# Value and output weights of a cross attention multiplied in split form

## The chip, the cores and the metric

The kernel runs on one core of a Trainium2 chip. The metric is the device time of one execution in microseconds (us); lower is better.

## The reference, cut to what matters

The program is one layer: a gated cross attention (stage "a" of the kernel), a causal self attention (stage "b") and a mixture of experts (stage "m"). The change lies in stage a, which computes this:

```python
q = rmsnorm((layernorm(x) @ Wq) per head, gq)      # 16 heads of 128, 1024 tokens
k = rmsnorm((ctx @ Wk) per head, gk)
v = (ctx @ Wv) per head
attn = softmax(q k^T / sqrt(128))                  # 16 sequences of 64 tokens
out = concat(attn @ v) @ Wo
x = x + tanh(g_xattn) * out
```

Since attn @ (ctx @ Wv) @ Wo equals (attn @ ctx) @ (Wv @ Wo), the kernel multiplies Wv of a head by Wo of that head (128x128 by 128x256) once, and applies the product, called vo, to attn @ ctx.

## The kernel before

The 1024 tokens are done in two halves of 512. A stage runs over eight pairs of heads for each half: first stage a for half 0 and half 1, then stage b twice, then stage m twice. Each engine has its own program (`cross_pair(u)` for a pair u of stage a), and semaphores tie them together. The programs are pipelined: in the body of pair u, TensorE makes the scores of u, the attention output of the pair before (`prev`) and the queries and keys of the next one (`nxt`), and VectorE and GpSimd already split the weights of the one after (`after`).

**Split form.** Most matmuls take their operands as two float32r tiles, `hi` (the value rounded by a copy) and `lo` (the rest, raw minus hi). A product is then three matmuls: hi by hi, hi by lo and lo by hi. On GpSimd the helper `rest` (L1470) makes every `lo`. The product of value and output weights is not made so: `value_out` (L629 to L636) multiplies the loaded float32 tiles as they are, one matmul for each head, into `bank_k`. It is made only in the bodies of half 0 (`u.weighs_values`), so eight times; ScalarE (`take_value_out`) and VectorE (`split_value_out`) then turn it into `vo_hi` and `vo_lo`, which stay for half 1.

**The order in a body of stage a.** TensorE: norm_q, scores(u), context_values(prev), keys of nxt, queries of nxt (head 0), keys (head 1), output(prev, head 0), queries (head 1), output(prev, head 1), value_out(u), norm_k(nxt), turn_attn(u). output waits for `pv_lo`. ScalarE: root_k, log_q, root_q, take_context_values(prev), take_k, exponentials(u), squares of the keys and queries, take_value_out, log_k, take_rows. VectorE: scale_scores(u) (L1230, L1233, L1239), subtract_max (L1244), `pv_lo` of prev (L1215), normalise(u) (L1250 to L1254), then queries and casts of weights, split_value_out. GpSimd: rest of the key squares of nxt (`sq_k_lo`), then rests of the query and key weights of `after`.

**Loads.** SyncE issues all the weight loads of stage a. `raw_a2` of a head holds Wv and Wo of that head (192 KB), and is loaded for the next pair once `value_out` has read it; behind it in the queue stands `reload_a1`, the load of the query and key weights two pairs on.

Of the kernel before, what the change touches and what calls it, by code (L numbers as in the profile page):

```python
# [29 lines left out]
ACT = mybir.ActivationFunctionType  # L30
AX = mybir.AxisListType.X

P = 128
# [160 lines left out]
def flamingo_layer(nc, x, ctx_t, ctx, head_a, head_b, pair_v, chunk_m, small, out, shared_units):  # L194
    TOK, D = x.shape
# [35 lines left out]
    with ExitStack() as stack:  # L231
# [94 lines left out]
        def stage_sems(tag, names):  # L326

            return {n: sem(f"{tag}_{n}") for n in names.split()}

        A = stage_sems("a", "wq_hi wq_lo wk_hi wk_lo q_done k_done sq_q sq_k sq_k_hi sq_k_lo qt kt scores raw scaled max "  # L330
                       "sub exp sum inv norm t_done attn_t vo_done vo_hi vo_lo ssk_done ssq_done ln_q "
                       "ln_k r_k r_q pv_done pv_hi pv_lo wo_done")

# [70 lines left out]
        def _(sp):  # L404
# [59 lines left out]
                load_m2(Unit(plan, "m", 0, h))  # L464
            for n in range(1, HALVES * PAIRS):
                if n < PAIRS:
                    sp.wait_ge(A["vo_done"], n)
                    for h in range(2):
                        load_a2(numbered("a", n), h)
                if n + 2 < HALVES * PAIRS:  # L470
                    reload_a1(n + 2)
# [42 lines left out]
        def _(pe):  # L514
# [114 lines left out]
            def value_out(u):  # L629

                pe.wait_ge(A["kt"], u.of(1) + 2)
                for h in range(2):
                    pe.wait_ge(ld_a2[h], 16 * u.n)
                    last = nc.tensor.matmul(bank_k[:, h * D:(h + 1) * D], raw_a2[h][:, AV:AV + C], raw_a2[h][:, AO:AO + D],
                                            start=True, stop=True)
                last.then_inc(A["vo_done"], 1)  # L636

            def norm_q(u):
# [204 lines left out]
        def _(act_e):  # L843
# [124 lines left out]
            def take_head_values(u, h):  # L968
                act_e.wait_ge(B["pv_done"], u.of(h))
                nc.scalar.activation(pv_hi[:, h], value_bank(h)[:], ACT.Copy).then_inc(B["pv_hi"], 1)  # L970

            def take_value_out(u):
                act_e.wait_ge(A["vo_done"], u.n)
                nc.scalar.activation(vo_hi[:, 2 * u.i:2 * u.i + 2, :], bank_k[:].rearrange("p (h n) -> p h n", h=2),
                                     ACT.Copy).then_inc(A["vo_hi"], 1)
# [16 lines left out]
            def cross_pair(u):  # L992

                prev, nxt = u.prev(), u.next()
                root_k(u)
                log_q(u)
                root_q(u)
                if prev:
                    take_context_values(prev)
                take_k(nxt, 0)  # L1000
                exponentials(u)
                if nxt.kind == "a":
                    square_k(nxt, 0, sq_k, A["sq_k"])
                    square_k(nxt, 0, sq_k_hi, A["sq_k_hi"])
                    take_k(nxt, 1)
                    square_k(nxt, 1, sq_k, A["sq_k"])
                    square_k(nxt, 1, sq_k_hi, A["sq_k_hi"])
                    square_q(nxt, 0)
                prepare(u)
                if nxt.kind == "a":  # L1010
                    square_q(nxt, 1)
                    if u.weighs_values:
                        take_value_out(u)
                    if u.very_first:
                        split_context(1)
                    prepare(u, 1)
                    log_k(nxt)
                take_rows(u)
                if nxt.kind != "a":
                    take_v(nxt, False)  # L1020
                    take_context_values(u)
                    take_k(nxt, 1)
# [443 lines left out]
        @block.gpsimd  # L1466
        def _(pool):
            def rest(lo, raw, hi, signal):

                nc.gpsimd.tensor_tensor(lo, raw, hi, ALU.subtract).then_inc(signal, 1)  # L1470

            def split_queries(u, h):
                if u.kind == "a":
                    pool.wait_ge(A["wq_hi"], u.of(h))
                    rest(wq_lo[h][:], raw_a1[h][:, AQ:AQ + D], wq_hi[h][:], A["wq_lo"])
                else:
                    pool.wait_ge(B["wq_hi"], u.of(h))
                    rest(wq_lo[h][:], raw_b1[h][:, 0:D], wq_hi[h][:], B["wq_lo"])

            def split_keys(u, h):  # L1480
                if u.kind == "a":
                    pool.wait_ge(A["wk_hi"], u.of(h))
                    rest(wk_lo[h][:, 0:P], raw_a1[h][:, AK:AK + P], wk_hi[h][:, 0:P], A["wk_lo"])
                else:
                    pool.wait_ge(B["wk_hi"], u.of(h))
                    rest(wk_lo[h][:], raw_b1[h][:, D:2 * D], wk_hi[h][:], B["wk_lo"])

            def split_gate_and_up(u):
                pool.wait_ge(M["wg_hi"], u.done())
                rest(wq_lo[u.parity][:], raw_m1[u.parity][:, MG:MG + D], wq_hi[u.parity][:], M["wg_lo"])  # L1490
                pool.wait_ge(M["wu_hi"], u.done())
                rest(wk_lo[u.parity][:], raw_m1[u.parity][:, MU:MU + D], wk_hi[u.parity][:], M["wu_lo"])

            def split_down(u):
                pool.wait_ge(M["wd_hi"], u.done())
                rest(wo_lo[u.parity][:], raw_m2[u.parity][:], wo_hi[u.parity][:], M["wd_lo"])

            def split_head(after, h):

                if after.kind == "m":  # L1500
                    split_gate_and_up(after.next() if h else after)
                else:
                    split_queries(after, h)
                    split_keys(after, h)

            def split_values(u):
                pool.wait_ge(B["wv_hi"], u.n)
                rest(wv_lo[:], raw_v[:], wv_hi[:], B["wv_lo"])

            def split_out(u, h):  # L1510
                pool.wait_ge(B["wo_hi"], u.of(h))
                rest(wo_lo[h][:], raw_b2[h][:], wo_hi[h][:], B["wo_lo"])

            def split_squares(u, h):
                pool.wait_ge(A["sq_k"], u.of(h))
                pool.wait_ge(A["sq_k_hi"], u.of(h))
                rest(sq_k_lo[:, h], sq_k[:, h], sq_k_hi[:, h], A["sq_k_lo"])

            def cross_pair(u):
                nxt = u.next()  # L1520
                after = nxt.next()
                if nxt.kind == "b":
                    split_values(nxt)
                if nxt.kind == "a":
                    for h in range(2):
                        split_squares(nxt, h)
                for h in range(2):
                    split_head(after, h)
                if u.very_first:
                    pool.wait_ge(ctxt_hi_ready, HALVES)  # L1530
                    rest(ctxt_lo[:, HT:TOK], ctxt[:, HT:TOK], ctxt_hi[:, HT:TOK], ctxt_lo_ready)

            def self_pair(u):
                nxt = u.next()
                after = nxt.next()
                if nxt.kind == "b":
                    split_values(nxt)
                    split_head(after, 0)
                for h in range(2):
                    split_out(u, h)  # L1540
                if nxt.kind == "b":
                    split_head(after, 1)

            def chunk(u):
                nxt = u.next()
                after = nxt.next() if nxt else None
                if u.very_first:
                    split_down(u)
                if after:
                    split_gate_and_up(after)  # L1550
                if nxt:
                    split_down(nxt)

            nc.gpsimd.memset(zeros[:].bitcast(F32), 0.0).then_inc(setup_pool, 1)
            nc.gpsimd.memset(ones[:], 1.0).then_inc(setup_pool, 1)
            nc.gpsimd.memset(attn_t[:], 0.0).then_inc(setup_pool, 1)
            nc.gpsimd.memset(eps5[:], 1e-5).then_inc(setup_pool, 1)
            nc.gpsimd.memset(eps6[:], 1e-6).then_inc(setup_pool, 1)
            nc.gpsimd.memset(ones_of[:].bitcast(F32), 0.0).then_inc(setup_pool, 1)
            pool.wait_ge(setup_pool, SETUP - SPB)  # L1560
            for s in range(SPB):
                nc.gpsimd.memset(ones_of[:, s, s * SEQ:(s + 1) * SEQ].bitcast(F32), 1.0).then_inc(setup_pool, 1)
            start = plan.first_of(0)
            for h in range(2):
                split_head(start, h)
            for h in range(2):
                split_squares(start, h)
            for h in range(2):
                split_head(start.next(), h)
            bodies = {"a": cross_pair, "b": self_pair, "m": chunk}  # L1570
            for kind, half in STAGES:
                run_units(pool, kind, half, bodies[kind])
# [70 lines left out]
```

## Time and profile before

| | us |
|---|---|
| median of 3 runs | 691.06 |
| lowest and highest | 689.58, 694.18 |
| profiled execution, whole time | 690.55 |
| its span, first to last instruction | 688.8 |
| TensorE busy in the span | 668.5 |
| VectorE busy | 470.1 |
| ScalarE busy | 340.9 |
| GpSimd busy | 297.5 |

The profile is of one execution; outside its span lie 1.75 us. Its mean granted TensorE clock is 0.998 of full speed. Times of a row are counted from the begin of the span. Stage a of half 0 runs from some 20 to 125 us, with a body each 13.07 us where nothing else is put beside it. Two bodies are longer, 13.79 us from 70.84 and 13.93 us from 84.63, as VectorE prepares the tokens of the second half in them; the first one is 11.60 us. A body is counted here from the start of its first VectorE instruction (`sc_sub` L1230).

### The profile page before, as it was taken

How to read it: one execution, taken by the hardware profiler on the slowest of the kernel's cores; microseconds unless marked ns; L12 is line 12 of the kernel's file. 1: busy time of each engine (PE TensorE's matmuls, PEld its weight loads, DVE VectorE, ACT ScalarE, POOL GpSimd, SP SyncE). 2: the span in 40 equal slices, each digit the busy share in tenths (PEclk: the TensorE clock that was granted, in tenths of full speed). 3: DMA queues.
4: the chain of work that ended last, by engine and by line, in shares of the span. 5: the costliest groups of instructions: out<-in, count | busy, mean ns of one | idle time of the engine just before them, and what ended most of it. 6: DMA issues, size and time to landing. Idle time of an engine off the chain costs nothing.

```text
span 688.8 us, 14632 instructions
## 1 busy us (share of the span) xinstructions
PE 668.5 (97%) x5415; PEld 585.9 (85%) x5415; DVE 470.1 (68%) x885; ACT 340.9 (49%) x689; POOL 297.5 (43%) x371
## 2 busy tenths in 40 slices
PE   7899999999999999999999999999998999999997
PEld 5688878887888899888989989888887988888886
DVE  5677877678786658676566668846556787655555
ACT  5676666676673333433353433354447444444443
POOL 4434224334334243434333335434553666655553
PEclk9999999999999999999999999999999999999999
DMA  6511311100102122222222212012332223332332
GB/s 205 178 47 52 88 47 48 48 25 24 43 6 57 44 86 63 78 62 62 78 87 68 77 47 77 31 32 70 91 93 87 74 83 92 102 92 91 91 91 92
DMA packets 35866, 50.08 MB, mean 73 GB/s; under 512 B 4064, under 2 KB 22880, under 8 KB 35808
## 3 DMA queue, kind: packets, MB, share of 16 engines
q1 hardware_dynamic: 35376, 48.89, 23.9%
q8 instruction: 39, 0.64, 0.4%
q10 hardware_dynamic: 432, 0.39, 0.2%
q14 instruction: 19, 0.16, 0.1%
HBM read 48.22 MB, written 1.05 MB: 72 GB/s over the span
## 4 chain that ended last, share of the span: by engine, by line
PE 75%; DVE 15%; ACT 5%; issue 2%; DMA 1%; POOL 1%; SPq 0%; DVEq 0%; ACTq 0%; POOLq 0%
PE acc L548 21%; PE bank_q L521 11%; PE bank_k L521 10%; PE bank_v L624 7%; PE bank_v L521 6%; PE bank_s L670 5%; PE bank_s L521 4%; PE bank_p L701 2%; PE bank_t L701 2%; PE bank_q L645 2%; DVE pv_lo L1215 2%; PE bank_p L656 2%; PE bank_t L678 2%; DVE sc L1233 2%; DVE sc_max L1239 2%
## 5 line engine op out<-in xcount | busy, mean ns | idle before, releaser
L548 PE MATMUL acc<-wo_hi,pv_hi 128*128 128x256 f32 x328 | 95.0, 290 | 2.6 <-DVE pv_lo L1335 2.1
L548 PE MATMUL acc<-wo_lo,pv_hi 128*128 128x256 f32 x328 | 93.1, 284 | 0.0
L548 PE MATMUL acc<-wo_hi,pv_lo 128*128 128x256 f32 x328 | 92.8, 283 | 0.0
L1470 POOL TENSOR_TENSOR sq_k_lo<-sq_k,sq_k_hi 128x512 fp32r<-128x512 f32 x32 | 42.2, 1320 | 105.3 <-ACT sq_k_hi L915 105.3
L1470 POOL TENSOR_TENSOR wq_lo<-raw_m,wq_hi 128x256 fp32r<-128x256 f32 x50 | 44.1, 882 | 65.4 <-DVE wq_hi L1291 61.2
L548 PEld LDWEIGHTS acc<-wo_hi,pv_hi 128*128 128x128 f32 x328 | 62.1, 189 | 6.8 <-issue 2.9
L548 PEld LDWEIGHTS acc<-wo_lo,pv_hi 128*128 128x128 f32 x328 | 62.4, 190 | 1.8
L1335 DVE TENSOR_TENSOR pv_lo<-rows_t,pv_hi 128x512 fp32r<-128x512 f32 (+1 forms) x51 | 36.8, 723 | 39.1 <-ACT pv_hi L990 39.1
L990 ACT ACTIVATE pv_hi<-rows_t 128x512 fp32r<-128x512 f32 (+1 forms) x51 | 31.7, 623 | 63.6 <-DVE rows_t L1330 62.0
L548 PEld LDWEIGHTS acc<-wo_hi,pv_lo 128*128 128x128 f32 x328 | 62.5, 191 | 0.0
L911 ACT ACTIVATE kt<-bank_k 128x512 f32<-128x512 f32 x64 | 38.0, 594 | 44.9 <-PE bank_k L521 44.9
L1470 POOL TENSOR_TENSOR wq_lo<-raw_b,wq_hi 128x256 fp32r<-128x256 f32 x32 | 24.5, 764 | 82.2 <-DVE wq_hi L1275 82.2
L521 PE MATMUL bank_q<-xt_hi,wq_hi 128*128 128x512 f32 x146 | 59.7, 409 | 0.1
L1322 DVE TENSOR_TENSOR r_k<-ln_k,unit_w 128x512 f32<-128x512 f32 x44 | 32.7, 743 | 37.7 <-ACT ln_k L981 37.5
L521 PE MATMUL bank_q<-xt_hi,wq_lo 128*128 128x512 f32 x146 | 57.5, 394 | 0.0
L521 PE MATMUL bank_q<-xt_lo,wq_hi 128*128 128x512 f32 x146 | 57.4, 393 | 0.0
L1470 POOL TENSOR_TENSOR wk_lo<-raw_m,wk_hi 128x256 fp32r<-128x256 f32 x50 | 41.3, 827 | 32.2 <-ACT wk_hi L1059 32.2
L521 PE MATMUL bank_k<-xt_hi,wk_hi 128*128 128x512 f32 x114 | 46.4, 407 | 0.0
L947 ACT ACTIVATE ex<-sc_sub 128x512 f32<-128x512 f32 x32 | 20.2, 632 | 52.1 <-DVE sc_sub L1244 52.1
L521 PE MATMUL bank_k<-xt_lo,wk_hi 128*128 128x512 f32 x114 | 44.9, 394 | 0.0
L521 PE MATMUL bank_k<-xt_hi,wk_lo 128*128 128x512 f32 x114 | 44.8, 393 | 0.0
L548 PE MATMUL acc<-vo_hi,pv_hi 128*128 128x256 f32 x128 | 37.7, 294 | 5.8 <-DVE pv_lo L1215 5.8
(203 smaller groups left out, 1985.2 us busy)
## 6 DMA issues: line engine op xcount, KB each, us to landing
raw_m<-in_chunk_m SPq DMA_DIRECT2D x50, 256.0 KB, 2.7
raw_a<-in_head_a SPq DMA_DIRECT2D x48, 192.0 KB, 2.6
raw_b<-in_head_b SPq DMA_DIRECT2D x32, 256.0 KB, 3.0
raw_m<-in_chunk_m SPq DMA_DIRECT2D x50, 128.0 KB, 2.1
raw_v<-in_pair_v SPq DMA_DIRECT2D x16, 256.0 KB, 2.9
raw_b<-in_head_b SPq DMA_DIRECT2D x32, 128.0 KB, 2.1
xs<-in_x SPq DMA_DIRECT2D x6, 128.0 KB, 3.1
out<-xs SPq DMA_DIRECT2D x3, 256.0 KB, 2.4
```

What stands on the lines that cost most here:

```text
L521: last = nc.tensor.matmul(bank[:], w[:, cols], m(k), start=n == 0, stop=n == 3 * chunks - 1)
L548: last = nc.tensor.matmul(acc[t // 2][:, (t % 2) * D:(t % 2 + 1) * D], w[:, tok], m, start=begins and n == 0, stop=True, skip_group_check= ...
L624: last = nc.tensor.matmul(bank_v[:, b * PAIR:(b + 1) * PAIR], m, w[:, cols], start=n == 0, stop=n == 3 * KD - 1)
L645: last = nc.tensor.matmul(bank_q[s * SEQ:(s + 1) * SEQ, h * NT + t:h * NT + t + 1], sq_q[:, h, b * SEQ:(b + 1) * SEQ], ones[:], start=True ...
L670: last = nc.tensor.matmul(bank_s[s * SEQ:(s + 1) * SEQ, g * SEQ:(g + 1) * SEQ], qt[:, h, tok], kt[:, h, tok], start=True, stop=True)
L701: last = nc.tensor.matmul(value_bank(h)[:, n * P:(n + 1) * P], vs[:, n, h * P:(h + 1) * P], attn_t[:, h * NT + n, :, :], start=True, stop= ...
L911: nc.scalar.activation(kt[:, h], bank_k[:], ACT.Copy).then_inc(stage["kt"], 1)
L947: nc.scalar.activation(ex[:], sc_sub[:], ACT.Exp).then_inc(stage["exp"], 1)
L990: nc.scalar.activation(pv_hi[:, u.parity, part], hh[:, part], ACT.Copy).then_inc(M["hh_hi"], 1)
L1322: nc.vector.tensor_tensor(gu, gs, weights, ALU.mult).then_inc(M["weighted"], 1)
L1335: nc.vector.tensor_tensor(pv_lo[:, u.parity, part], hh[:, part], pv_hi[:, u.parity, part], ALU.subtract)\
L1470: nc.gpsimd.tensor_tensor(lo, raw, hi, ALU.subtract).then_inc(signal, 1)
```

## The change

In half 0, the loaded value and output weights are split before they are multiplied. ScalarE rounds them (two activations for each head, behind root_q), GpSimd takes the rests (two subtractions for each head, first in its body), and TensorE makes three float32r matmuls for each head where there was one in float32. The split value weights lie in the unused upper half of `wk_hi` and `wk_lo`, the output weights in `wo_hi` and `wo_lo`, which stage a did not use. `raw_a2` is free again when GpSimd has read it, and no longer when TensorE has.

```diff
-        A = stage_sems("a", "wq_hi wq_lo wk_hi wk_lo q_done ...
+        A = stage_sems("a", "wq_hi wq_lo wk_hi wk_lo vw_hi vw_lo q_done ...
...
             for n in range(1, HALVES * PAIRS):
                 if n < PAIRS:
-                    sp.wait_ge(A["vo_done"], n)
                     for h in range(2):
+                        sp.wait_ge(A["vw_lo"], 2 * numbered("a", n - 1).of(h))
                         load_a2(numbered("a", n), h)
...
                 pe.wait_ge(A["kt"], u.of(1) + 2)
                 for h in range(2):
-                    pe.wait_ge(ld_a2[h], 16 * u.n)
-                    last = nc.tensor.matmul(bank_k[:, h * D:(h + 1) * D], raw_a2[h][:, AV:AV + C], raw_a2[h][:, AO:AO + D],
-                                            start=True, stop=True)
+                    pe.wait_ge(A["vw_lo"], 2 * u.of(h))
+                    v_hi, v_lo = wk_hi[h][:, P:2 * P], wk_lo[h][:, P:2 * P]
+                    for n, (w, m) in enumerate(((v_hi, wo_hi), (v_hi, wo_lo), (v_lo, wo_hi))):
+                        last = nc.tensor.matmul(bank_k[:, h * D:(h + 1) * D], w, m[h][:], start=n == 0, stop=n == 2)
                 last.then_inc(A["vo_done"], 1)
...
+            def split_value_weights(u):            # ScalarE
+                if u.n > 1:
+                    act_e.wait_ge(A["vo_done"], u.n - 1)
+                for h in range(2):
+                    act_e.wait_ge(ld_a2[h], 16 * u.n)
+                    nc.scalar.activation(wo_hi[h][:], raw_a2[h][:, AO:AO + D], ACT.Copy).then_inc(A["vw_hi"], 1)
+                    nc.scalar.activation(wk_hi[h][:, P:2 * P], raw_a2[h][:, AV:AV + C], ACT.Copy).then_inc(A["vw_hi"], 1)
...
                 root_q(u)
+                if u.weighs_values:
+                    split_value_weights(u)
                 if prev:
                     take_context_values(prev)
...
+            def split_value_weights(u):            # GpSimd
+                for h in range(2):
+                    pool.wait_ge(A["vw_hi"], 2 * u.of(h) - 1)
+                    rest(wo_lo[h][:], raw_a2[h][:, AO:AO + D], wo_hi[h][:], A["vw_lo"])
+                    pool.wait_ge(A["vw_hi"], 2 * u.of(h))
+                    rest(wk_lo[h][:, P:2 * P], raw_a2[h][:, AV:AV + C], wk_hi[h][:, P:2 * P], A["vw_lo"])
...
                 after = nxt.next()
+                if u.weighs_values:
+                    split_value_weights(u)
                 if nxt.kind == "b":
                     split_values(nxt)
```

## Rows read from the trace of the kernel before

**Rows 1.** The page: the chain that ended last by engine, and one load.

```profile
PE 75%; DVE 15%; ACT 5%; issue 2%; DMA 1%; POOL 1%; SPq 0%; DVEq 0%; ACTq 0%; POOLq 0%
...
raw_a<-in_head_a SPq DMA_DIRECT2D x48, 192.0 KB, 2.6
```

**Rows 2.** Waits from 31 to 131 us: total us, times, longest us.

```profile
PEld acc L548 <- DVE pv_lo L1215: 6.1, 8, 1.4
```

**Rows 3.** Chain in order of time, 55 to 82 us: start us, us, what.

```profile
60.04 0.69 DVE sc_sub L1244
60.73 1.21 DVE pv_lo L1215 x2
...
66.48 0.86 PE bank_k L634 x4
```

**Rows 4.** Timeline of TensorE around value_out: start us, us, instruction.

```profile
66.20 0.28 PE L548 MATMUL acc<-vo_hi,pv_lo 128*128 128x256 f32 x1
66.32 1.03 PE L634 MATMUL bank_k<-raw_a 128*128 128x256 f32 x4
67.00 0.58 PE L656 MATMUL bank_p<-sq_k_hi,ones_of 128*128 128x512 f32 x1
67.42 0.39 PE L656 MATMUL bank_p<-sq_k_lo,ones_of 128*128 128x512 f32 x1
...
68.11 0.60 PE L678 MATMUL bank_t<-sm,attn 128*128 128x128 f32 x4
```

**Rows 5.** Timeline of VectorE in the body that begins at 70.84 us.

```profile
70.84 0.69 DVE L1230 TENSOR_TENSOR sc_sub<-bank_s,r_k 128x512 f32<-128x512 f32 x1 [2.14 <-PE bank_s L670]
71.64 0.69 DVE L1233 TENSOR_TENSOR sc<-sc_sub,r_q 128x512 f32<-128x512 f32 x1
...
73.08 0.69 DVE L1244 TENSOR_TENSOR sc_sub<-sc,sc_max 128x512 f32<-128x512 f32 x1
73.69 0.68 DVE L1215 TENSOR_TENSOR pv_lo<-bank_p,pv_hi 128x512 fp32r<-128x512 f32 x1
...
75.84 1.63 DVE L1254 TENSOR_TENSOR attn<-ex,ex_inv 128x512 f32<-128x512 f32 x1
```

**Rows 6.** Timeline of GpSimd in the same body, its first instruction.

```profile
75.63 1.30 POOL L1470 TENSOR_TENSOR sq_k_lo<-sq_k,sq_k_hi 128x512 fp32r<-128x512 f32 x1 [7.52 <-ACT sq_k_hi L915]
```

**Rows 7.** Timeline of ScalarE in the same body.

```profile
70.19 0.21 ACT L938 ACTIVATE r_q<-ln_q 128x8 f32<-128x8 f32 x1
71.86 0.60 ACT L965 ACTIVATE pv_hi<-bank_p 128x512 fp32r<-128x512 f32 x1 [1.46 <-PE bank_t L691]
```

**Rows 8.** Instructions of lines L1470 and L1059: ns min/median/max, first and last start.

```profile
L1470 POOL TENSOR_TENSOR wq_lo<-raw_a,wq_hi x32: 722/734/1317, 6.8 to 197.8; 128x256 fp32r<-128x256 f32 x32
L1470 POOL TENSOR_TENSOR wk_lo<-raw_a,wk_hi x32: 448/461/513, 7.5 to 198.5; 128x128 fp32r<-128x128 f32 x32
...
L1059 ACT ACTIVATE wk_hi<-raw_m x50: 402/408/439, 447.8 to 677.3; 128x256 fp32r<-128x256 f32 x50
```

**Rows 9.** Timeline of GpSimd, then of VectorE, 470 to 474 us.

```profile
471.71 0.74 POOL L1470 TENSOR_TENSOR wk_lo<-raw_m,wk_hi 128x256 fp32r<-128x256 f32 x1
472.41 1.19 POOL L1470 TENSOR_TENSOR wo_lo<-raw_m,wo_hi 128x256 fp32r<-128x256 f32 x1
...
471.86 1.14 DVE L1322 TENSOR_TENSOR r_k<-ln_k,unit_w 128x512 f32<-128x512 f32 x1
473.03 0.69 DVE L1330 TENSOR_TENSOR rows_t<-bank_s,r_k 128x512 f32<-128x512 f32 x1
```

**Rows 10.** Timeline of GpSimd, then of VectorE, 295 to 298 us.

```profile
295.56 1.48 POOL L1470 TENSOR_TENSOR wo_lo<-raw_b,wo_hi 128x256 fp32r<-128x256 f32 x2
...
295.67 0.70 DVE L1163 TENSOR_SCALAR st<-ms 128x4 f32<-128x4 f32 x1
```

**Rows 11.** Timeline of TensorE in the first body, 25 to 32 us.

```profile
27.91 0.47 PE L656 MATMUL bank_p<-sq_k_hi,ones_of 128*128 128x512 f32 x1 [1.55 <-POOL sq_k_lo L1470]
```

**Rows 12.** Chain in order of time, 84 to 90 us.

```profile
83.98 0.73 DVE hn L1158 x2
```

More of the change, by code:

```diff
@@ L328, in stage_sems @@
             return {n: sem(f"{tag}_{n}") for n in names.split()}
-        A = stage_sems("a", "wq_hi wq_lo wk_hi wk_lo q_done k_done sq_q sq_k sq_k_hi sq_k_lo qt kt scores raw scaled max "
+        A = stage_sems("a", "wq_hi wq_lo wk_hi wk_lo vw_hi vw_lo q_done k_done sq_q sq_k sq_k_hi sq_k_lo qt kt scores raw scaled max "
                        "sub exp sum inv norm t_done attn_t vo_done vo_hi vo_lo ssk_done ssq_done ln_q "
```

## Prediction

> **What bounds the kernel now.** I began with the chain that ended last: 75% of it is TensorE and 15% VectorE, GpSimd has 1% [rows 1]. Then I read the chain over two bodies of stage a. It goes from the scores into VectorE, through `sc_sub`, `sc`, `sc_max`, `sc_sub` and the two `pv_lo`, and from there over TensorE's outputs, queries, value_out, norm_k, turn, norm_q and scores back to VectorE [rows 3]. TensorE's weight loads wait for `pv_lo` eight times in eight bodies, 6.1 us in all [rows 2]. So two things count in a body of 13.07 us: what TensorE issues between `pv_lo` and the scores, and the time from the scores to `pv_lo` on VectorE. What delays one of the four score instructions delays the whole body. ScalarE and GpSimd have gaps.
>
> **TensorE's part.** The two float32 matmuls show as four records. On the chain they stand with 0.86 us [rows 3]. The first starts at 66.32, norm_k's matmuls at 67.00 and 67.42, and turn_attn at 68.11 [rows 4]; three matmuls of norm_k lie in 68.11 - 67.42 = 0.69, so one takes 0.23. After the change six float32r matmuls of 256 columns take their place. Their nearest row is output's matmul just ahead, of the same shape and with new weights each time: 66.20 to 66.32, 0.12 each [rows 4]. The turn would then start at 66.32 + 6 x 0.12 + 4 x 0.23 = 67.96, 0.15 us earlier than 68.11. The work is small, and three matmuls are more instructions than one: the gain is 0.15 and not two thirds. It could be nothing, if the new matmuls do not keep to 0.12, and it is at most 0.3 if the drain behind the float32 pair (67.00 to 67.42, 0.42 against 0.23) goes in full besides 0.86 - 0.72. It counts in six bodies of eight. In the first one TensorE waits 1.55 us for `sq_k_lo` behind value_out [rows 11], and in the fifth VectorE, with `hn` up to 84.71, comes later than the scores [rows 12]. Sum: 6 x 0.15 = 0.9 us gained.
>
> **ScalarE's part.** Four activations are put in behind root_q, which starts at 70.19 and takes 0.21; the next, `pv_hi`, starts at 71.86 after 1.46 us of idle time [rows 7]. A 128x256 copy takes 0.41 [rows 8]. For 128x128 on ScalarE there is no such row here; it lies between 0.21, for 128x8 [rows 7], and 0.41. One after another with no overlap that is 1.24 to 1.64 us, so at the very worst 0.2 us beyond the gap; I take 0.3 for each small one and the usual overlap, some 1.2 us, and so nothing. What is queued behind is `pv_hi` and then the keys and the exponentials; `pv_lo` cannot run before VectorE has done `subtract_max` at 73.69 [rows 5], and `pv_hi` of 71.86 is ready by 72.46, so even 0.2 us stays covered. The cover is TensorE's context_values; without it the whole 1.2 us would go to `pv_hi`. The waits added to ScalarE are for value_out of the pair before, long done, and for the load.
>
> **GpSimd's own time.** Added are two rests of 0.73 and two of 0.46 in each body, 2.4 us [rows 8]. GpSimd waits 7.52 us for `sq_k_hi` before its first instruction [rows 6]: none of its later work moves, and even held by VectorE the last rest is made by some 74, while value_out comes at 66.32 + 13.07 = 79.4 [rows 4], so TensorE's new wait costs nothing. By time in the queue this is free.
>
> **What GpSimd does to VectorE.** It is not free by place. `attn` in this body takes 1.63 us where the same shape takes 0.69 in `sc` and `sc_sub` [rows 5]: it starts at 75.84, while `sq_k_lo` runs from 75.63 to 76.93 [rows 6], and ends at 77.47, 0.54 after it. Both read two SBUF tiles. The same is seen with shorter ones: `r_k<-ln_k,unit_w`, issued at 471.86 beside a GpSimd subtraction that ends at 472.45, ends at 473.00, 0.55 after it, and GpSimd's next one is now held, 1.19 in place of 0.74, ending 0.60 after VectorE's [rows 9]. `rows_t<-bank_s,r_k`, with one operand in PSUM, keeps its 0.69 beside it. So the two engines take turns, and an instruction that has waited needs 0.55 (VectorE, 512 columns) or 0.60 (GpSimd, 256) more. Between two GpSimd subtractions that follow each other a waiting VectorE instruction gets in: `st` at 295.67 ends at 296.37, not at 297.04 [rows 10].
>
> Today nothing of GpSimd lies beside `sc` and `sc_sub`. Now the four rests begin when `wo_hi` is there, and this is the score chain's time. Worked out for the body at 70.84, with the first activation at 70.35 and its result at 70.76: rest 1 from 70.85, rest 2 (0.46) from 0.70 later, 71.55 to 72.01. `sc` comes at 71.64, is held, and ends at 72.01 + 0.55 = 72.56 in place of 72.33. Rest 3 ends 0.60 later, 73.16. `sc_max` reads one tile and is not held, 72.59 to 73.28. Rest 4 starts at 73.12 and ends at 73.58, so the second `sc_sub`, due at 73.31, ends at 74.13 in place of 73.77. That is 0.36 on the chain; I take 0.35. With GpSimd 0.15 later the same steps give about 0.13, so the value hangs on a tenth of a microsecond. The lower bound is 0. The upper bound, two rests of 256 columns each met at their start, is 2 x (0.74 - 0.14) = 1.2, with 0.14 as the part of its 0.69 that a waiting instruction does not repeat. For the sixth body, in which `hn` keeps the chain up to 84.71 [rows 12] and `sc` comes later to the rests, I take 0.2. The delay counts in the first and the fifth body as well, since `ex` and the key squares hang on `sc_sub`. Sum: 7 x 0.35 + 0.2 = 2.65 us lost.
>
> **SyncE's part.** The load of `raw_a2` leaves when GpSimd has read it, early in the body, at some 74, and lands 2.6 us later [rows 1], nearly 7 us before ScalarE reads it in the next body (70.35 + 13.07 = 83.4). Behind it waits `reload_a1`, for rests that GpSimd makes late in the body as before; it was issued only after value_out, and may go a little earlier. Nothing of either is late: 0, and no gain either, as nobody waits for these loads in steady state.
>
> **Sum.** 2.65 - 0.9 = 1.75 us more: the profiled execution goes from 690.55 to 692.3. The median of the runs, 691.06, lies 0.5 above it; the median after I put at 692.8.
>
> **A rule beside the row.** The Trainium skill, "SBUF — State Buffer", section "Who interferes with whom", says that a VectorE instruction with two SBUF inputs and a GpSimd instruction that reads SBUF exclude each other, the one that comes second blocking fully until the other ends. It speaks against this change, and the trace agrees that they exclude each other (1.63 against 0.69). Taken literally, the blocked one runs its whole 0.69 behind the other's end, and the trace shows 0.55. By the rule a body would lose 0.36 + 2 x 0.14 and more, as rest 3 too would end later.
>
> **The rivals.**
> - No collisions that matter. `sc` and `sc_sub` get in first each time, as the rests' begin hangs on a tenth of a microsecond. Only TensorE's gain is left: 691.06 - 0.9 = 690.2. Against it: four rests fill 2.3 us of the 2.9 us from 70.85 to 73.77, and both two-tile instructions lie in that time.
> - Full serial blocking. Each blocked VectorE instruction needs 0.69 behind the other's end, with two in a body 0.28 more, and the held rest 3, ending 0.14 later, adds as much: 8 x 0.42 = 3.4, so 692.8 + 3.4 = 696.2. The rule of the page named above would bring this. The 0.55 of [rows 9] speaks against it.
> - Slower: VectorE does not get in between rests that are ready one behind the other. `sc` then waits for all four: 70.85 + 0.70 + 0.42 + 0.70 + 0.46 = 73.13, and ends at 73.68 in place of 72.33, 1.35 in each of eight bodies, 10.8 - 0.9 = 9.9, so 701. It decides if two or more rests in a row win; [rows 9, 10] show the turn taken after each. It becomes a matter of over 1% from 0.98 us for each body.
> - The change does not give what it says: the six matmuls take as long as before or more (0.14 each instead of 0.12). Then the 0.9 fall away: 693.7.
>
> **How the numbers follow.** Forecast, alternating collisions, 691.5 to 694: 0.50. No collisions: 0.20. Full blocking or meetings at the worst place, 694 to 698: 0.15. All four in a row: 0.07. No gain on TensorE: 0.06; the rest, 0.02, is a gain of a size that I can't derive. The range leaves out most of the 701 case and the edge of the others: 689.9 to 697. What a measurement here can tell from no change is about 1%, 6.9 us: slower than 698 takes the case of 701 and a little of the third, 0.09; faster than 684.2 would need the whole float32 product to vanish in each body, 0.02; within 1% 0.89.
>
> **What would show it.** Right: `sc` L1233 and `sc_sub` L1244 with medians over 0.75 in half 0 but 0.69 in half 1; `wo_lo<-raw_a` partly over 1.1; L634 as 48 records of 256 columns with a turn 0.15 earlier; `pv_hi` still waiting for TensorE; bodies of some 13.27. Wrong: L1233 at 0.69 throughout (first rival), or at 1.5 and more (third), or `pv_hi` no longer released by TensorE.

## The result, and the profile after

The median is 695.71 us over 13 runs (693.33 to 699.36) against 692.03 over 13 runs of the kernel before. The ratio is 1.006, with an interval from 1.0039 to 1.0081: the change makes the kernel slower by 0.4 to 0.8%, under the 1% at which the chances were drawn. The profiled execution took 696.09 us, with a span of 694.3.

The stretches of the bodies in half 0, after (columns: stretch, its length, busy us and count of each engine, granted clock, DMA share, GB/s; the second is the body from 34.63):

```profile
20.18:34.63 14.45, 11.43 (x98) 9.25 (x99) 7.72 (x14) 9.84 (x23) 10.17 (x13) 0.80 0.60 198
34.63:47.87 13.24, 13.24 (x138) 11.56 (x140) 9.87 (x16) 9.06 (x20) 6.26 (x10) 0.96 0.21 61
47.87:61.05 13.18, 12.65 (x138) 10.96 (x139) 9.84 (x16) 9.65 (x23) 7.68 (x11) 1.00 0.22 62
61.05:74.26 13.21, 12.68 (x138) 10.99 (x139) 9.83 (x17) 9.64 (x23) 7.67 (x11) 1.00 0.22 61
74.26:89.42 15.16, 14.63 (x157) 12.63 (x156) 14.52 (x34) 11.46 (x28) 9.62 (x14) 1.00 0.19 53
89.42:104.74 15.32, 13.12 (x127) 11.73 (x127) 10.58 (x20) 9.21 (x21) 5.36 (x8) 0.89 0.18 52
```

and the three long or odd ones of them before:

```profile
20.05:31.65 11.60, 9.11 (x96) 7.11 (x98) 7.35 (x15) 7.94 (x16) 6.44 (x7) 1.00 0.76 230
...
70.84:84.63 13.79, 13.54 (x150) 11.74 (x148) 13.14 (x34) 8.92 (x19) 4.93 (x6) 1.00 0.23 67
84.63:98.56 13.93, 12.97 (x134) 11.17 (x132) 10.44 (x20) 9.59 (x19) 4.93 (x6) 1.00 0.17 50
```

A common body grew from 13.07 to 13.18 or 13.21. Three grew by far more: the first by 2.85, the fifth by 1.37 and the sixth by 1.39. The first, the second (13.24 us) and the sixth show a granted clock under 1, which no body had in the profile before: part of each ran at the lower level of TensorE's clock. The sixth shows it in both profiles of the change, the first in one only. The other profile of the same kernel (taken with the last experiments, mean clock 0.998) has these two:

```profile
19.76:31.73 11.97, 8.94 (x98) 7.20 (x99) 7.73 (x14) 9.05 (x22) 9.23 (x12) 1.00 0.72 225
...
86.50:101.88 15.38, 13.18 (x127) 11.79 (x127) 10.66 (x20) 9.33 (x21) 5.33 (x8) 0.89 0.18 52
```

So 2.5 of the first body's 2.85 us belong to a fall of the clock that does not come each time, and 0.4 (11.97 against 11.60) to the change.

**VectorE in the fifth body, after**, which answers to [rows 5]:

```profile
75.06 0.84 DVE L1244 TENSOR_TENSOR sc<-sc_sub,r_q 128x512 f32<-128x512 f32 x1
75.93 0.69 DVE L1250 TENSOR_REDUCE sc_max<-sc 128x8 f32<-128x512 f32 x1
76.65 0.81 DVE L1255 TENSOR_TENSOR sc_sub<-sc,sc_max 128x512 f32<-128x512 f32 x1
77.39 0.68 DVE L1226 TENSOR_TENSOR pv_lo<-bank_p,pv_hi 128x512 fp32r<-128x512 f32 x1
```

and GpSimd beside it:

```profile
74.21 0.73 POOL L1481 TENSOR_TENSOR wo_lo<-raw_a,wo_hi 128x256 fp32r<-128x256 f32 x1 [2.54 <-ACT wo_hi L978]
74.89 0.46 POOL L1481 TENSOR_TENSOR wk_lo<-raw_a,wk_hi 128x128 fp32r<-128x128 f32 x1
75.31 1.20 POOL L1481 TENSOR_TENSOR wo_lo<-raw_a,wo_hi 128x256 fp32r<-128x256 f32 x1
76.46 0.46 POOL L1481 TENSOR_TENSOR wk_lo<-raw_a,wk_hi 128x128 fp32r<-128x128 f32 x1
```

The two engines take turns. Rest 2 ends at 75.35 and `sc` at 75.90; rest 3 is held and ends 0.61 behind `sc`; rest 4 ends at 76.92 and `sc_sub` at 77.46. The steps of 0.55 and 0.60 taken from [rows 9] hold to 0.01.

**TensorE's product, after**, which answers to [rows 4]:

```profile
69.75 0.28 PE L548 MATMUL acc<-vo_hi,pv_lo 128*128 128x256 f32 x1
69.87 0.28 PE L636 MATMUL bank_k<-wo_hi,wk_hi 128*128 128x256 f32 x1
...
70.59 0.39 PE L657 MATMUL bank_p<-sq_k_hi,ones_of 128*128 128x512 f32 x1
...
71.53 0.60 PE L679 MATMUL bank_t<-sm,attn 128*128 128x128 f32 x4
```

From the first matmul of the product to the turn it is 1.66 us, against 68.11 - 66.32 = 1.79 before: 0.13 gained, with six matmuls in 0.72.

**What was not foreseen: `hn`.** VectorE's four `hn` at the end of the fifth body, and GpSimd beside them with the rests of the sixth:

```profile
87.01 2.49 DVE L1169 TENSOR_SCALAR hn<-xs,mv,st 128x256 f32<-128x256 f32 x4
```

```profile
87.41 0.73 POOL L1481 TENSOR_TENSOR wo_lo<-raw_a,wo_hi 128x256 fp32r<-128x256 f32 x1 [0.85 <-ACT wo_hi L978]
88.10 0.50 POOL L1481 TENSOR_TENSOR wk_lo<-raw_a,wk_hi 128x128 fp32r<-128x128 f32 x1
88.56 0.79 POOL L1481 TENSOR_TENSOR wo_lo<-raw_a,wo_hi 128x256 fp32r<-128x256 f32 x1
89.31 0.51 POOL L1481 TENSOR_TENSOR wk_lo<-raw_a,wk_hi 128x128 fp32r<-128x128 f32 x1
```

Before, with nothing of GpSimd beside them, they took 1.38 together:

```profile
83.33 1.38 DVE L1158 TENSOR_SCALAR hn<-xs,mv,st 128x256 f32<-128x256 f32 x4
```

TensorE then waits for the sixth body's `pv_lo` at length, and comes back slow (its timeline):

```profile
91.00 0.40 PE L521 MATMUL bank_k<-ctxt_hi,wk_lo 128*128 128x512 f32 x1
93.59 0.47 PE L548 MATMUL acc<-vo_hi,pv_hi 128*128 128x256 f32 x1 [2.20 <-DVE pv_lo L1226]
93.86 0.42 PE L548 MATMUL acc<-vo_lo,pv_hi 128*128 128x256 f32 x1
94.08 0.42 PE L548 MATMUL acc<-vo_hi,pv_lo 128*128 128x256 f32 x1
```

The outputs follow each other at 0.21 in place of 0.12, the pace of 1.2 GHz where the rest runs at 2.4.

**Times by clock.** Each run has a mean granted clock, so runs can be compared at equal clock. The runs of both kernels whose clock is on record (91 of before, beside the experiments, and 24 of the change):

| mean clock | before: runs, mean us | change: runs, mean us | difference |
|---|---|---|---|
| 1.0 | 32, 689.76 | none | |
| 0.998 | 32, 690.87 | 4, 693.28 | 2.41 |
| 0.995 | 10, 692.24 | 6, 694.61 | 2.37 |
| 0.993 | 1, 693.66 | 9, 695.89 | 2.23 |
| 0.985 to 0.99 | 14, 694.64 (0.99); 2, 696.31 (0.988) | 1, 697.07 (0.989); 1, 698.91 (0.988); 3, 699.29 (0.985) | |
| all | 91, 691.36 | 24, 695.74 | 4.38 |

At one clock the change costs 2.2 to 2.4 us. The other 2.0 of the 4.38 come from a lower mean clock, 0.9930 against 0.9969. The kernel before shows what such a fall is worth: its runs at 0.99 took 4.9 us more than those at 1.0, which makes some 1.9 us for a difference of 0.0039 (an estimate).

The same mean clock does not say that the clock fell in the same place. The profile before, at 0.998, has its fall in stage m:

```profile
535.00:540.00 5.00, 5.00 (x25) 4.71 (x25) 3.70 (x9) 3.46 (x4) 2.15 (x4) 0.66 0.26 79
```

The second profile of the change, at 0.998 too, has its fall in the sixth body and none in stage m. Its eight bodies took 108.52 us against 104.64, 3.9 more, while the span is only 2.6 us longer. So the 2.4 us at 0.998 are the change with its own fall in the sixth body, less a fall that the runs of before had elsewhere. Against the runs of before at 1.0 the change costs 3.5 us there (693.28 against 689.76). What it costs without any fall is seen below, in the change with zeros at 1.0: 2.3 us. (0.89 over the 15.3 us of the sixth body makes a mean of 0.998, so runs at 1.0 had no such fall; this is worked out and no trace of such a run was kept.)

### The profile page after: what moved, and what is told of

The parts are those of the page before. It is cut to its first block, busy times and chain, and to the rows that moved or that the text cites. A ratio compares the mean times of both kernels' runs of the same rounds, so it can differ in the third digit from the quotient of the medians.

```text
span 694.3 us, 14735 instructions
## 1 busy us (share of the span) xinstructions
PE 671.4 (97%) x5431; PEld 589.5 (85%) x5431; DVE 473.8 (68%) x885; ACT 349.5 (50%) x721; POOL 318.8 (46%) x403
## 4 chain that ended last, share of the span: by engine, by line
PE 76%; DVE 15%; ACT 5%; issue 3%; POOL 1%; DVEq 0%; ACTq 0%; POOLq 0%
PE acc L548 21%; PE bank_q L521 11%; PE bank_k L521 10%; PE bank_v L624 7%; PE bank_v L521 6%; PE bank_s L671 5%; PE bank_s L521 4%; PE bank_q L646 2%; PE bank_p L702 2%; PE bank_t L702 2%; PE bank_p L657 2%; PE bank_t L679 2%; DVE pv_lo L1226 2%; DVE sc L1244 2%; DVE sc_sub L1255 2%
```

## The experiments

Eleven kernels, in three groups of four, four and three, each group on one chip. Ratios are to runs of the kernel before in the same group.

**The splits alone.** TensorE keeps the float32 product.

```diff
+                        sp.wait_ge(A["vo_done"], n)               # beside the wait for vw_lo
...
-                    pe.wait_ge(A["vw_lo"], 2 * u.of(h))
-                    for n, (w, m) in enumerate(((v_hi, wo_hi), (v_hi, wo_lo), (v_lo, wo_hi))): ...
+                    pe.wait_ge(ld_a2[h], 16 * u.n)
+                    last = nc.tensor.matmul(... raw_a2[h][:, AV:AV + C], raw_a2[h][:, AO:AO + D], start=True, stop=True)
```

> The splits of the change are made on ScalarE and GpSimd, but the product is the float32 one of before; what they make is not used. Theory (GpSimd's rests hold VectorE's two-tile instructions and hn in the fifth body): sc and sc_sub stay at 0.8 to 1.0 us in half 0, hn at 2.5 us, and the kernel is 3 to 5 us slower than before, since TensorE's 0.15 us a body is missing. Rival (the product in split form costs, by its matmuls or by a TensorE clock that falls as it has less work): within 1.5 us of before. Clock: if the lighter product brings the half clock in the second body, it is not seen here.

Measured: 1.0061 (1.0035 to 1.0088), and at equal clock 2.9 us over before at 1.0 (one run, 692.46 against 689.52), 2.5 at 0.998, and 2.3 and 2.1 at 0.993 and 0.99. The third body:

```profile
45.08:58.44 13.36, 12.84 (x136) 11.03 (x137) 9.82 (x17) 9.64 (x23) 7.66 (x11) 1.00 0.22 65
```

13.36 against 13.07: the collisions cost 0.29 in a body. `hn` took 1.93, and not the 2.5 expected, as the rests began 0.54 us behind its start and not 0.40; the last of them then held `sc` of the sixth body, 0.87. The splits carry the whole loss. The low clocks came here too (5 runs of 8 at 0.993 or less), although the product is the old one; so they do not need the lighter product.

**The product alone.** The weights are split in the first body only; all eight products are made from these halves, so seven are of the wrong weights.

```diff
-                if u.weighs_values:
+                if u.very_first:
                     split_value_weights(u)          # on ScalarE and on GpSimd
...
+                    if n == 1:
+                        sp.wait_ge(A["vw_lo"], 4)
+                    sp.wait_ge(A["vo_done"], n)
...
-                    pe.wait_ge(A["vw_lo"], 2 * u.of(h))
+                    pe.wait_ge(A["vw_lo"], 2 * (h + 1))
+                    pe.wait_ge(ld_a2[h], 16 * u.n)
```

> The weights are split only in the first body, and all eight products are made from those halves, so all but the first are of the wrong heads' weights. Theory: six bodies each 0.15 us shorter, the first one longer by its collisions, in sum 0.5 us faster to 0.5 slower than before as long as the clock holds, up to 2.5 slower if the half clock still comes in the second body. Rival (the product costs): 3 to 4 us slower, as the change.

Measured: 1.002 (0.9996 to 1.0045); at equal clock 0.0 (1.0) and 0.4 us (0.998, 0.995) below before. The second body:

```profile
32.03:44.97 12.94, 12.69 (x138) 10.98 (x139) 9.56 (x17) 8.63 (x17) 4.96 (x6) 1.00 0.22 63
```

12.94 against 13.07, so 0.13 to 0.15 gained in a body. The fifth body did not gain:

```profile
70.80:84.90 14.10, 13.85 (x153) 12.02 (x153) 12.51 (x34) 9.08 (x20) 5.27 (x6) 1.00 0.22 68
```

It took 14.10 where it took 13.79 before, though no rest of the splits lies in it. `attn` now started ahead of `sq_k_lo` and kept 0.69 us in place of 1.63, and the cast `wq_hi` met `sq_k_lo` and took 0.81 in place of 0.51. The median of 692.55 against 690.89 is the clock's: 6 runs of 12 had 0.993 or less.

**ScalarE alone.** Its four activations without the rests, with the float32 product.

```diff
-                        sp.wait_ge(A["vw_lo"], 2 * numbered("a", n - 1).of(h))
+                        sp.wait_ge(A["vw_hi"], 2 * numbered("a", n - 1).of(h))
+                        sp.wait_ge(A["vo_done"], n)
...
-                if u.weighs_values:
-                    split_value_weights(u)          # GpSimd's
```

> Only ScalarE's four activations are added, without rests, with the float32 product of before; what they make is not used. Theory: within 0.5 us of before, pv_hi still released by TensorE. Rival (ScalarE's queue): 2 to 4 us slower.

Measured: 1.0002 (0.998 to 1.0023), with common bodies of 13.04 to 13.08. ScalarE's part costs nothing, and the rival of its queue falls. The profile has a clock of 0.87 in the first body and 0.993 in all, with none of GpSimd's rests and none of the new matmuls.

**The rests held behind subtract_max.** One wait on GpSimd moves its four rests off the score instructions.

```diff
             def split_value_weights(u):             # GpSimd's
+                pool.wait_ge(A["sub"], u.n)
                 for h in range(2):
```

> The whole change, but GpSimd's rests wait for subtract_max of the same body, so that they lie beside pv_lo, ex_sum and attn and not beside sc, sc_sub and hn. Theory: sc and sc_sub back at 0.69 us, hn at 1.4, attn at 2 us or more without cost, bodies of 12.9 us; the kernel 1 us faster than before, and 4 to 5 us faster than the change; if the half clock stays in the second body, only 2 to 3 faster than the change. Rival (ScalarE's four activations delay what stands behind them): as slow as the change, 3.5 us over before.

Measured: 1.0028 (1.0008 to 1.0048), a median of 693.69. The groups of VectorE in half 0 are as expected (count, busy us, mean ns):

```profile
L1244 DVE TENSOR_TENSOR sc<-sc_sub,r_q 128x512 f32<-128x512 f32 x9 | 6.2, 693 | 0.9
L1255 DVE TENSOR_TENSOR sc_sub<-sc,sc_max 128x512 f32<-128x512 f32 x9 | 6.2, 692 | 0.3
L1169 DVE TENSOR_SCALAR hn<-xs,mv,st 128x256 f32<-128x256 f32 x4 | 1.4, 408 | 0.0
```

Bodies took 12.92 us. But the first took 13.57, with a clock of 0.87, and 8 of 12 runs had a mean clock of 0.993 or less. At equal clock it is 0.0 to 0.4 us under before, not 1: the fifth body took 14.25 in place of 13.79, since `sq_k_lo` now met the cast `wq_hi`, 0.97 in place of 0.51, in a body that VectorE bounds. Most of this is not the rests': the product alone, with none there, has 14.10 and 0.81. The expectation of a gain failed in the median, by the clock; that of 2 to 3 us under the change, if the half clock stayed, held at its edge (2.0, against a median from other runs).

**Zeros for TensorE in the first body.** With the change, with the held rests, and with the kernel before, the same edit:

```diff
                     if u.weighs_values:
                         value_out(u)
+                    if u.very_first:
+                        pe.wait_ge(A["raw"], 1)
+                        for _ in range(6):
+                            nc.tensor.matmul(bank_s[:], zeros[:, 0:P], zeros[:], start=True, stop=True)
```

> The change with six matmuls of zeros (0.23 us each) behind value_out in the first body only, where TensorE waits 1.7 us for sq_k_lo. Theory (part of the change's time is TensorE's half clock in the second body, which follows that wait): the first body is 11.9 to 12.1 us again, mean clocks of the runs 0.995 and more, and the median is 1 to 2.5 us below the change, 1.5 to 3 us over before. Rival (the half clock comes anywhere, by chance): clocks spread down to 0.985 to 0.99 as in the change, 3.5 to 4.5 us over before.

> The change with the rests held behind subtract_max and the same six matmuls of zeros in the first body. Theory: collisions and the half clock of the second body both gone, 0.3 to 1.5 us faster than before. Rival (half clock by chance): 2 to 3 us slower than before, as with held rests alone.

> The kernel before with the same six matmuls of zeros in the first body. If the half clock of the second body also takes part of the executions of before: clocks under 0.995 become rare and the median falls by 0 to 1.5 us. If not: no difference.

Measured: the change with zeros 1.0023 (1.0000 to 1.0047); held rests with zeros 0.9991 (0.9972 to 1.0009); before with zeros 0.9998 (0.9980 to 1.0016). TensorE around the zeros in the change:

```profile
26.16 1.55 PE L775 MATMUL bank_s<-zeros 128*128 128x512 f32 x6
28.05 0.47 PE L657 MATMUL bank_p<-sq_k_hi,ones_of 128*128 128x512 f32 x1 [0.33 <-POOL sq_k_lo L1485]
28.36 0.39 PE L657 MATMUL bank_p<-sq_k_lo,ones_of 128*128 128x512 f32 x1
```

The wait of 1.7 us shrinks to 0.33, and the matmuls behind it keep 0.23. The first body took 12.00 us, as the change's own does where its clock holds (11.97). The change with zeros met what was expected of it: 11 of 12 runs at 0.995 or more, the median 2.7 us over before. Held rests with zeros did not: its median is that of before (690.72 against 690.70) and not 0.3 to 1.5 below. Of the 24 runs of the two kernels without the sixth body's trouble (held rests, and before) none had a mean clock under 0.995; of the 91 runs of before without zeros 17 had, and of the 12 of held rests 8. With the two kernels further below, five kernels had zeros, and 1 of their 60 runs was under 0.995. The zeros show that the half clock of the first two bodies depends on TensorE's idle time there. They made the kernel before no faster in the median, as most of its runs had no mean clock under 0.995 anyway. The change with zeros still costs 2.3 us at equal clock (692.04 against 689.77).

**The sixth body's rests held, two ways.** First behind the first score instruction, which follows `hn`:

```diff
+                if u.i == 5:
+                    pool.wait_ge(A["raw"], u.n)
```

> The change, with GpSimd's rests of the sixth body alone held until VectorE's first score instruction is through, so that hn (2.5 us in the profile of the change, 1.4 before) meets none of them. Theory: hn 1.4 us, fifth body 13.9 to 14.1 us instead of 15.2, no half clock behind it in the sixth; 1 us faster than the change at the same clock, 2 us in the median. Rival: hn stays over 2 us for another reason.

Measured: 1.0059 (1.0036 to 1.0083), a median as that of the change, and nothing gained at equal clock (693.22 against 693.28 at 0.998). `hn` is well again, but the rests now meet the next two:

```profile
87.74 1.38 DVE L1169 TENSOR_SCALAR hn<-xs,mv,st 128x256 f32<-128x256 f32 x4
89.03 0.69 DVE L1241 TENSOR_TENSOR sc_sub<-bank_s,r_k 128x512 f32<-128x512 f32 x1
89.82 1.27 DVE L1244 TENSOR_TENSOR sc<-sc_sub,r_q 128x512 f32<-128x512 f32 x1
91.12 0.69 DVE L1250 TENSOR_REDUCE sc_max<-sc 128x8 f32<-128x512 f32 x1
91.84 0.81 DVE L1255 TENSOR_TENSOR sc_sub<-sc,sc_max 128x512 f32<-128x512 f32 x1
```

The fifth body was 14.05 as expected, the sixth 16.09 with the half clock still in it. The expectation failed: it gave a place where `hn` was safe and not where the chain was. So the second way, with zeros in the first body and behind subtract_max:

```diff
+                if u.i == 5:
+                    pool.wait_ge(A["sub"], u.n)
```

> The change with zeros in the first body, and the sixth body's rests alone held behind subtract_max, so that neither hn nor the score instructions of that body meet them. Theory: hn 1.4 us, fifth body near 14.1, sixth near 13.8 to 13.9 with no half clock; at full clock 1.3 us below the change with zeros, so 1 us over before. Rival (hn's 1.1 us is hidden, or the half clock of the sixth body has another cause): a difference under 0.5 us, or the half clock stays.

Measured: 1.0016 (0.9999 to 1.0032). Its fifth and sixth body:

```profile
72.00:86.05 14.05, 13.53 (x153) 11.70 (x149) 13.40 (x34) 10.41 (x25) 7.48 (x10) 1.00 0.20 56
86.05:99.80 13.75, 12.66 (x134) 11.08 (x134) 10.07 (x19) 10.13 (x22) 7.67 (x11) 1.00 0.20 60
```

The change with zeros had 15.15 and 15.34 there. At a clock of 0.998 it is 1.4 us over before (692.33 against 690.90), where the change with zeros was 2.4 over; at 1.0 it is 0.75 over (two runs, 690.66 against 689.91), where the other was 2.3 over. So holding these rests is worth 1.0 at 0.998 and 1.4 at 1.0 (690.66 against 692.04; 1.3 was expected), and 1.10 of it is seen in the fifth body, which is `hn`.

**The change again, and the best of it.** The change itself beside the last two, and a kernel with held rests in all bodies but the first and the fifth, with zeros:

```diff
+                if u.i not in (0, 4):
+                    pool.wait_ge(A["sub"], u.n)
```

> The change itself, unaltered, beside the two others on one chip. If the half clock is part of what it costs, its runs again spread down to clocks of 0.985 to 0.99, with the median 3.5 to 5 us over before, against 2.3 us at equal clock.

> The best that the runs so far point to: rests held behind subtract_max in all bodies but the first and the fifth, where holding them put 0.5 us on the chain (they then meet sq_k_lo in the first and a weight cast in the fifth), and the six matmuls of zeros in the first body. Theory: at full clock 0.1 to 0.3 us faster than before and 0.3 faster than with all held; in the median 0.3 to 1 us faster than before. Rival: no better than all held with zeros.

Measured: the change 1.0068 (1.0045 to 1.0091), clocks from 0.998 down to 0.985, 693.27 at 0.998 against 690.90. Its median is 5.1 us over that of before, at the upper end of what was expected. The other one 0.998 (0.9961 to 1.0000), a median of 689.77 against 690.73, and 0.25 and 0.40 us under before at clocks of 1.0 and 0.998; against held rests in all bodies (0.4 over before at 1.0, 0.1 under at 0.998) it is 0.3 to 0.7 better. It is the fastest of all, with common bodies of 12.91 to 12.93. Its interval just touches no change.

## Why the prediction was right, point by point

The time lies in the range, and the sign, the mechanism and its two steps (0.55 and 0.60) were right. The sum was not: 1.75 was forecast, 2.2 to 2.4 is measured at equal clock and 3.7 to 5.1 with the clock, by the runs that are compared. The median of 695.71 lies 2.9 over the forecast of 692.8 and outside the 691.5 to 694 that the prediction gave to its own mechanism; it fell where full blocking or the worst meetings were put, and it was neither.

- TensorE's part: 0.15 in a body forecast, 0.13 to 0.15 measured, by the product alone and by the change.
- ScalarE's part and GpSimd's own time at nothing: right. SyncE's at nothing: nothing in the profiles speaks against it, but it was not tested alone. ScalarE alone gave 1.0002; its small copies took 0.29 (0.3 was taken), and `pv_hi` is still released by TensorE, now after 0.45 us.
- The collisions: 0.35 in a body forecast, 0.27 to 0.29 measured (13.36 against 13.07, and 0.15 + 0.12 in the rows of the fifth body). The steps were right; the first rest came 0.06 earlier against `sc_sub` than was worked out.
- In the fifth body the prediction's own collisions came to 0.26 (14.05 against 13.79, where `hn` was kept free).
- The term that was mis-sized is the one for the sixth body, "in which `hn` keeps the chain up to 84.71 and `sc` comes later to the rests, I take 0.2". The rests did not meet `sc` but `hn`, and it cost 1.1 in place of 0.2. [Rows 10] held the evidence: the `st` of 295.67 is a TENSOR_SCALAR with one tile input, and was held beside a rest. The prediction used that row for the order of turns, and asked only of instructions with two SBUF inputs whether they collide. Summed with measured values: first body 0.4, five common bodies and the fifth body's own 6 x 0.28 = 1.7, `hn` 1.1, less 6 x 0.14 = 0.8, is 2.4. The change with zeros measured 2.3 at a clock of 1.0.
- The clock was no term at all. The prediction treated lengthened waits of TensorE as their own length. With the change stretches at the lower level came more often (14 of 24 runs under 0.995, against 17 of 91), 2.0 us in the mean of the runs. The range held the result only because it had been drawn wide for other cases.
- The rivals: no collisions, and four rests in a row, are refuted by the rows of the fifth body, and no gain on TensorE by the product alone. Full serial blocking is refuted too: what was held ended 0.54 behind the other and not 0.69. By that literal reading of the Trainium skill ("SBUF — State Buffer", "Who interferes with whom") it would be 696.2, which lies near the median by chance. The same section counts some instructions with one SBUF input among those that hold the shared ports, copies, casts and `tensor_scalar` in a two-port mode; `hn` is a `tensor_scalar`, and that it was held, 2.49 against 1.38, agrees with it. Its pace does not: one `hn` took 0.41 us where the cast `wq_hi` of the same 128x256 took 0.28. Which mode it ran in no run here shows, and so it stays open why it is held.

**What stays open.** Which part of the change brings the low clocks more often: with 8 to 12 runs each, the splits alone (5 of 8 at 0.993 or less), the product alone (6 of 12) and the held rests (8 of 12) all had many, ScalarE alone (3 of 12) had as before (17 of 91). The zeros show that idle time in the first body matters, not how much each part adds. The wait for `sq_k_lo` alone does not decide it: with 1.70 us of it the clock fell in one profile of the change and with 1.71 held in the other, and with 1.55 it fell with ScalarE alone and held before. In the sixth body the clock fell in the four profiles with a wait of 1.78 to 2.20 us for `pv_lo`, and held with 1.67 (the splits alone) and less; that it follows from the wait was not tested apart. Falls in stage m stand in profiles of before and of the change's variants alike, and their cause was not sought. The edit that would split the rests ahead of the score chain, in the gap behind `vo_lo`, was not tried.

## What to carry to other kernels

Work that is moved to an engine with much idle time has to be checked against what the other engines do at the same moment: GpSimd's 2.4 us were free by its queue, and cost 0.28 us a body and 1.1 us once, because they lay beside VectorE's chain and not 3 us later. Before a shared resource is priced, list every instruction of the chain in the stretch, also those of one input, and look up one row for each kind beside the intruder. Where TensorE already waits, compare runs at equal mean clock first, and look in the traces where the clock fell, as a mean does not say it; otherwise a loss of 2 us and a clock that falls more often look alike.

## What the runs showed of the hardware

- VectorE's `tensor_scalar` from one SBUF tile to another, four times 128x256, took 1.38 us alone, 1.93 or 2.49 beside GpSimd's subtractions.
- A GpSimd subtraction that waited for VectorE ended 0.61 us behind it (128x256), and a held 128x512 instruction of VectorE 0.54 behind GpSimd's; both leave out a part of their own 0.73 and 0.69.
- Six matmuls of zeros, 1.4 us of work in a wait of 1.7 us, kept the clock of the first bodies: with them no run of before or of held rests was under 0.995 in 24, against 17 in 91 and 8 in 12 without them; in all kernels with zeros it was 1 in 60.
